# Short down products of two pairs in one section, eight result buffers, goals formed between two pairs' stores

## What is computed

```python
top_p, top_i = jax.lax.top_k(probs, TOPK)                 # 8 experts, 2 for each token
h1 = jnp.einsum('nc,efc->enf', xf, expert_fc1)            # 176 hidden columns
h2 = jnp.einsum('nc,efc->enf', xf, expert_fc2)
out_e = jnp.einsum('enf,ecf->enc', silu(h1) * h2, expert_proj)
y = jnp.einsum('ne,enc->nc', combine, out_e)
s = silu(xf @ shared_fc1.T) * (xf @ shared_fc2.T) @ shared_proj.T
y = y + sigmoid(xf @ shared_gate_w.T) * s
x = x + gb * y
```

## Time and profile before

| | us |
|---|---|
| median of 3 runs | 369.16 (369.09 to 369.76) |
| the profiled execution | 370.18 |
| its span (first to last instruction) | 368.4 |
| PE busy | 353.6 (96%) |
| DVE / ACT / POOL busy | 239.1 / 158.3 / 140.8 |

### The profile page before, as it was taken

One profiled execution on the slowest core, in us unless ns is written; L12 is line 12 of the kernel. 1 busy time (PEld: TensorE's weight loads), 2 busy tenths in 40 slices (PEclk: granted clock), 3 DMA queues, 4 the chain that ended last, 5 costly groups with the idle time before them and its releaser, 6 DMA issues.

```text
span 368.4 us, 9813 instructions
## 1 busy us (share of the span) xinstructions
PE 353.6 (96%) x3793; PEld 218.3 (59%) x3794; DVE 239.1 (65%) x578; ACT 158.3 (43%) x303; POOL 140.8 (38%) x207
## 2 busy tenths in 40 slices
PE   8999999999999998999999999989889999999996
PEld 8445656575656575556845754656556666664464
DVE  3199584998799679756393693136556666665485
ACT  3597628634872622271052411135555555531110
POOL 7706006201712162225363076502465656665000
PEclk9999999999999999999999999999999999999999
DMA  6980300000000000079921062233545554531694
GB/s 194 352 248 5 117 4 3 2 4 4 3 2 4 4 2 4 4 215 285 304 77 59 1 171 80 102 59 72 116 103 117 119 116 103 116 81 45 195 356 135
DMA packets 51660, 36.66 MB, mean 100 GB/s; under 512 B 31447, under 2 KB 48290, under 8 KB 51620
## 3 DMA queue, kind: packets, MB, share of 16 engines
q1 hardware_dynamic: 48212, 27.58, 28.3%
q0 software_dynamic: 3408, 8.51, 7.2%
HBM read 18.06 MB, written 13.68 MB: 86 GB/s over the span
## 4 chain that ended last, share of the span: by engine, by line
PE 70%; issue 9%; POOL 6%; SPq 6%; ACT 4%; DMA 2%; DVE 1%; another core or an unknown queue 1%; DVEq 0%; POOLq 0%; ACTq 0%
PE at_ps L1899 9%; PE work L1570 7%; PE at_ps L1521 7%; PE work L1521 6%; POOL xs_sorted L682 4%; SPq L515 4%; PE work L1922 4%; PE work L1711 3%; PE at_ps L1570 3%; PE work L1761 3%; PE work L1924 3%; PE work L1536 2%; PE at_ps L1536 2%; PE at_ps L1608 2%; PE o_even L1664 2%
## 5 line engine op out<-in xcount | busy, mean ns | idle before, releaser
L1899 PE MATMUL at_ps<-arena 128*128 x156 | 54.5, 473 | 1.3 <-DVE arena L1425 1.3
L715 POOL DMA_INDIRECT ys_tokens<-er_pos,goal_u x39 | 39.7, 1018 | 19.7 <-issue 9.1
L682 POOL DMA_INDIRECT xs_sorted<-h2tok,pos_u x32 | 33.0, 1032 | 21.5 <-issue 12.2
L966 ACT ACTIVATE arena<-h2tok 128x512 uint16<-128x512 uint16 x39 | 30.3, 777 | 24.0 <-DMA h2tok<-xs_sorted 23.2
L1899 PEld LDWEIGHTS at_ps<-arena 128*128 128x128 f32 x156 | 26.6, 190 | 16.6 <-issue 8.1
L1445 DVE SCALAR_TENSOR_TENSOR er_pos<-work,goal,sq 128x256 f32<-128x256 f32 x39 | 17.5, 481 | 18.4 <-PE work L1929 11.9
L627 POOL TENSOR_TENSOR arena<-arena 128x512 f32<-128x512 f32 x8 | 10.2, 1281 | 48.7 <-DVE arena L1377 48.7
L621 POOL COPY h2tok<-xn 128x2048 uint16<-128x2048 uint16 x4 | 7.6, 1892 | 48.0 <-DVE xn L1277 32.6
L1521 PE MATMUL work<-h2T,sup_sb 128*128 128x512 f32 x56 | 25.8, 600 | 0.0
L736 ACT ACTIVATE hs<-at_ps 128x512 f32<-128x512 f32 x10 | 6.0, 598 | 43.0 <-PE at_ps L1521 40.2
L1266 DVE COPY_PREDICATED arena<-causal,at_ps 128x512 f32<-128x512 uint32 x32 | 20.5, 725 | 4.0 <-PE at_ps L1608 4.0
(11 more groups left out here) (291 smaller groups left out, 797.8 us busy)
## 6 DMA issues: line engine op xcount, KB each, us to landing
arena<-ys_tokens SPq DMA_DIRECT2D x8, 512.0 KB, 7.7
arena<-in_e_up SPq DMA_DIRECT2D x8, 352.0 KB
x_sb<-in_x SPq DMA_DIRECT2D x4, 512.0 KB, 9.2
out_rows<-x_sb SPq DMA_DIRECT2D x16, 128.0 KB, 2.2
sup_sb<-in_s_up SPq DMA_DIRECT2D x2, 640.0 KB, 4.9
xs_sorted<-state SPq DMA_DIRECT2D x2, 526.0 KB
xs_sorted<-state SPq DMA_DIRECT2D x8, 131.5 KB
hs<-in_wmod SPq DMA_DIRECT2D x1, 1024.0 KB, 7.7
```

The costliest lines, as they stand in the source:

```text
L682: g.indirect_dma_start(out=xs_dram, out_offset=bass.IndirectOffsetOnAxis(ap=pos_u[:, k, t:t + 1], axis=0), in_=h2row[:, t, :], in_offset=N ...
L715: g.indirect_dma_start(out=ys_dram, out_offset=bass.IndirectOffsetOnAxis(ap=goal_u[:, i:i + 1], axis=0), in_=yout[:, q % 2, u, :], in_offs ...
L966: a.activation(xT[:, u % XBUFS, :].bitcast(U16).rearrange("p (k n a) -> p a k n", k=KC, a=2), xp[:, u, :, :].rearrange("p (a k) n -> p a k ...
L1899: ins = t_.matmul(at_ps[2 + u % 2][:, 0:2 * FE], xT[:, u % XBUFS, k * P:(k + 1) * P], eup[:, bass.ds(e, 1), k, :].rearrange("p a n -> p (a ...
```

## The change

Six things are edited.

1. PE: `down` keeps the main products only. Two pairs write into the two halves of each of the banks `work[0]` and `work[1]`; the new `down_short` does the short products of both pairs after the second one's main products, in the order even, odd, even, odd. PE waits for y once for two pairs.
2. DVE: the four y of a block come together behind that section (`out_rows`), in the next pair's iteration, and the four gains of a block together in its second pair's iteration, behind the two products. Gains lie in `xn` (four places), `yout` has eight buffers, each with a semaphore of its own.
3. POOL: `goals(q + 2)` moves from ahead of `put_rows(q)` to between `put_rows(q)` and `put_rows(q + 1)`.
4. ACT: `tail_odd` has four places, so its copy waits for a section two blocks back.
5. SP: the first eight tiles are loaded in the order four planes, four words, four planes, four words.
6. `mod_cols`: each product gets 128 columns (each batch column repeated 64 times), and DVE reads one of each 64.

The diff, cut to its core:

```diff
-        tail_odd = xn2[:, 0:2, :]
+        tail_odd = xn2[:, :, :]
-        row_step, row_gain = sq[:, 0, 0:HID], sq[:, 1, :].rearrange("p (a n) -> p a n", a=2)
-        yout = er_pos[:, :, :].rearrange("p a (t c) -> p a t c", t=2)
+        row_step, row_gain = sq[:, 0, 0:HID], xn
+        yout = [home[:, a, :].rearrange("p (t c) -> p t c", t=2) for home in (er_pos, h2T[:, 0, :, :]) for a in range(2)]
...
@@ sync
-            for u in range(0, EGRP, 2):
-                load_planes(u)
-                load_planes(u + 1)
-                load_words(u)
-                load_words(u + 1)
+            for u in range(0, EGRP, EGRP // 2):
+                for t in range(u, u + EGRP // 2):
+                    load_planes(t)
+                for t in range(u, u + EGRP // 2):
+                    load_words(t)
...
@@ gpsimd
             for q in range(0, EPAIRS, 2):
+                put_rows(q)
                 if q + 2 < EPAIRS:
                     goals(q + 2)
-                put_rows(q)
                 put_rows(q + 1)
...
@@ scalar
-                act.wait_ge(down_full, q - 1)
+                act.wait_ge(down_full, d)
...
-                            odd_rows(q0 + u // 2, u // 2, e[u])
+                            odd_rows(d0 + u // 4 - 1, u // 2, e[u])
...
@@ vector
             def row_gains(i, u):
-                if not isinstance(i, int) or i:
+                if u % 4 == 0 and (not isinstance(i, int) or i):
                     dve.wait_ge(y_out, i)
                 dve.wait_ge(goal_ready, i + 2)
...
-            def evac_y(i0, q0, u):
-                dve.wait_ge(down_full, q0 + u // 2 + 1)
+            def evac_y(i0, d0, u):
+                dve.wait_ge(down_full, d0 + u // 4 + 1)
...
+            def out_rows(i0, d0, u, tiles=4):
+                for n in range(u, u + tiles):
+                    y_slot_free(i0, n)
+                    evac_y(i0, d0, n)
...
                 for u in range(0, tiles, 2):
                     if u or not first:
                         evac_hT(q0 + u // 2 - 1, (u // 2 - 1) % XPAIRS)
                     expert_h(i0 + u, u)
-                    if u or not first:
-                        row_gains(i0 + u - 2 if u else i0 - 2, (u - 2) % EGRP)
                     if u + 1 < tiles:
                         expert_h(i0 + u + 1, u + 1)
-                    for t in range(2):
...
+                    if u == 4:
+                        out_rows(i0, d0, 0)
+                    elif u == 0 and not first:
+                        out_rows(i0 - EGRP, d0 - XPAIRS // 2, 4)
+                    elif u % 4 == 2:
+                        row_gains(i0 + u - 2, u - 2)
+                        row_gains(i0 + u, u)
...
             evac_hT(EPAIRS - 1, XPAIRS - 1)
-            row_gains(ETILES - 1, EGRP - 2)
-            y_slot_free(ESLOTS - EGRP, EGRP - 2)
-            evac_y(ESLOTS - EGRP, ESLOTS // 2 - XPAIRS, EGRP - 2)
+            out_rows(ESLOTS - EGRP, (ESLOTS // 2 - XPAIRS) // 2, 4, tiles=3)
...
@@ tensor
-                            ins = t_.matmul(o[:, (w * KC + h) * BATCH:(w * KC + h + 1) * BATCH], wmod_sb[:, k, c0:c0 + P],
-                                            csil[:, k, :], start=(k == 0), stop=(k == KC - 1))
+                            ins = t_.matmul(o[:, (w * KC + h) * P:(w * KC + h + 1) * P], wmod_sb[:, k, c0:c0 + P],
+                                            csil[:, k, :].unsqueeze(2).broadcast_to([P, BATCH, P // BATCH]),
+                                            start=(k == 0), stop=(k == KC - 1))
...
-                at_least(pe, y_out, i, 0)
+                if w % 2 == 0:
+                    at_least(pe, y_out, i, 0)
+                c = slice(w % 2 * HID, w % 2 * HID + HID)
                 for t in range(tiles):
...
+            def down_short(q, w, e, tiles=4):
+                if tiles == 4:
+                    pe.wait_ge(odd_ready, q + 1)
...
+                for a in range(2):
+                    c = slice(a * HID, a * HID + HID)
+                    ins = t_.matmul(work[0][:, c], hTe[0:FE1, a, 2 * P:3 * P],
+                                    edn[0:FE1, 1, bass.ds(e[2 * a], 1), :].rearrange("p a n -> p (a n)"),
+                                    start=False, stop=True, skip_group_check=True)
+                    if 2 * a + 1 < tiles:
+                        ins = t_.matmul(work[1][:, c], hTe[r, a, 2 * P:3 * P], tail_odd[r, (w - 1 + a) % XPAIRS, :],
+                                        start=False, stop=True, skip_group_check=True)
                 ins.then_inc(down_full, 1)
...
+                def short_behind(u):
+                    if u == 4:
+                        down_short(q0 + 1, 1, e[0:4])
+                    elif u == 0 and before is not None:
+                        down_short(q0 - 1, XPAIRS - 1, before)
...
                     pair_behind(down, u)
+                    short_behind(u)
```

More of the change, by code:

```diff
@@ L387, in adaln_moe @@
         hTp_full, hTe_ready, down_full, y_out, ys_stored = (
-            sem("hTp_full"), sem("hTe_ready"), sem("down_full"), sem("y_out"), [sem(f"ys_st{i}") for i in range(4)])
+            sem("hTp_full"), sem("hTe_ready"), sem("down_full"), sem("y_out"), [sem(f"ys_st{i}") for i in range(EGRP)])
         weights_ready, row_ready, end_ready = sem("weights_ready"), sem("row_ready"), sem("end_ready")
@@ L537, in _ @@
             for j, s in enumerate(ys_stored):
-                sp.wait_ge(s, 16 * len(range(j, ETILES, 4)))
+                sp.wait_ge(s, 16 * len(range(j, ETILES, EGRP)))
             for q in range(NBLK):
@@ L975, in _, with odd_rows, group @@
             ereg = [act.alloc_register(f"odd_expert{u}") for u in range(EGRP)]
-            def odd_rows(q, w, e):
-                act.wait_ge(down_full, q - 1)
+            def odd_rows(d, w, e):
+                act.wait_ge(down_full, d)
                 copy_odd_rows(w, e)
             def copy_odd_rows(w, e):
-                a.activation(tail_odd[CHUNK:CHUNK + FE1, w % 2, :], edn[0:FE1, 0, bass.ds(e, 1), :].rearrange("p a n -> p (a n)"),
+                a.activation(tail_odd[CHUNK:CHUNK + FE1, w, :], edn[0:FE1, 0, bass.ds(e, 1), :].rearrange("p a n -> p (a n)"),
                              ACT.Copy).then_inc(odd_ready, 1)
-            def group(i0, q0, tiles=EGRP, first=False, last=False):
+            def group(i0, d0, tiles=EGRP, first=False, last=False):
                 act.load(ereg, texp_u[0:1, bass.ds(i0, EGRP)])
@@ L994, in group @@
                     if u % 2:
-                        if first and u < 4:
+                        if first:
                             copy_odd_rows(u // 2, e[u])
                         else:
-                            odd_rows(q0 + u // 2, u // 2, e[u])
+                            odd_rows(d0 + u // 4 - 1, u // 2, e[u])
                     if not (last and u + XBUFS - 1 >= tiles):
@@ L1003, in _ @@
             with act.Fori(1, ESLOTS // EGRP - 1) as grp:
-                group(grp * EGRP, grp * XPAIRS)
-            group(ESLOTS - EGRP, ESLOTS // 2 - XPAIRS, tiles=ETILES - ESLOTS + EGRP, last=True)
+                group(grp * EGRP, grp * (XPAIRS // 2))
+            group(ESLOTS - EGRP, (ESLOTS // 2 - XPAIRS) // 2, tiles=ETILES - ESLOTS + EGRP, last=True)
             for f in range(FTS):
@@ L1918, in down @@
                     pe.wait_ge(shev_done, 2 * NBLK - 2)
[L1919 removed]
+                if w % 2 == 0:
+                    at_least(pe, y_out, i, 0)
+                c = slice(w % 2 * HID, w % 2 * HID + HID)
                 for t in range(tiles):
                     main = edn_odd if t else edn[:, 0, :, :]
[L1922 to L1930 removed]
+                    t_.matmul(work[t][:, c], hTe[:, w % 2, t * P:(t + 1) * P],
+                              main[:, bass.ds(e[t], 1), :].rearrange("p a n -> p (a n)"),
+                              start=(w % 2 == 0), stop=False, skip_group_check=True)
+            def down_short(q, w, e, tiles=4):
+                if tiles == 4:
+                    pe.wait_ge(odd_ready, q + 1)
+                else:
+                    pe.wait_ge(odd_ready, q)
+                r = slice(CHUNK, CHUNK + FE1)
+                for a in range(2):
[6 more added lines that the diff above has]
+                                        start=False, stop=True, skip_group_check=True)
                 ins.then_inc(down_full, 1)
@@ L1937, in fetch_experts @@
                 pe.load(ereg, texp_u[0:1, bass.ds(i0, EGRP)])
-            eprev = [pe.alloc_register(f"expert_prev{u}") for u in range(2)]
+            eprev = [pe.alloc_register(f"expert_prev{u}") for u in range(4)]
             def group(i0, q0, before=None, tiles=EGRP, last=False):
@@ L1948, in pair_behind @@
                     elif before is not None:
-                        step(i0 - 2, q0 - 1, XPAIRS - 1, before)
+                        step(i0 - 2, q0 - 1, XPAIRS - 1, before[2:4])
+                def short_behind(u):
[3 more added lines that the diff above has]
+                        down_short(q0 - 1, XPAIRS - 1, before)
```

(6 more changed lines are left out.)

40 lines of the change are left out of this document (13 added, 27 removed).

## The result

The changed kernel takes 374.38 us (median of 4 runs, 373.68 to 374.52) where the kernel before takes 369.12 (4 runs, 368.13 to 369.76): a ratio of 1.0129, 95% interval 1.0098 to 1.0161. It is slower, by less than 2%. (All ratios are formed over the runs in the fast state, and so need not be the quotient of the two medians, here 1.0143.) The profiled execution after took 373.68 us with a span of 371.9, so the two spans differ by 3.5 us. The granted clock of TensorE is 1.0 in both, from the first slice on.

What follows compares the result with a forecast made beforehand. TensorE bounds the kernel before at 8.78 us a block; afterwards a four-engine ring of 9.37 would bind. Loop, tail and reload delays end 3.3 later: 369.16 + 3.3 = 372.5 us, range 368.3 to 376.0.

Steps and rivals of the forecast that it cites:

- the ring (part 2): Experts' loop: result, two stores, goals, gains, copy, mains, shorts, result close a circle of 9.37 us a block.
- part 1: Short passes of two pairs in one section: 0.40 us less per two pairs, 4.0 us in all on PE.
- part 4: SP's first loads: first PE gap closes, pair 3 at 256.4 against 256.58, nothing gained; ends -1.0 and +0.5.
- first stretched ring: Start of the loop: second block's y at about 266.9, not 266.0, behind tile 11's late planes: +0.8 us.
- The tail: After the last pair: gains wait for goals; shared product 8.9 behind the pair, now 8.1; first reload at 348.2.
- the sum: Whole kernel: the delays of loop, tail and reload added up, putting the end 3.2 to 3.3 us later.
- part 3: Eight result buffers: DVE's wait of 1.48 us for a store's landing goes.
- part 5: Sixteen first-column passes widened from 2 to 128 columns: cost 0, bounds -0.1 to +0.4 us.
- A: Rival: goals come in time, PE stays the bound at 8.38 a block, 364 us; 0.15 with cases between it and D.
- B: Rival: "remote" stall of 1.49 recurs or reload lands at 7.7, not 5.5: 374 to 377 us; 0.14 with C.
- C: Rival: short passes don't stream, 0.32 each, ring grows by 0.2 a block: 374.1 us; 0.14 together with B.
- D: Rival: ring shorter by 0.3 to 0.5 a block, 368.5 to 370 us, about no change; 0.07.

Runs made afterwards that it cites:

- e1: Changed kernel with the next block's goals formed ahead of the block's four stores: 368.35 us, 0.9916 of the kernel before.
- e2: Changed kernel with the next block's goals formed behind all four stores: 405.15 us, 1.0909 of the kernel before.
- e3: Changed kernel with a block's four gains formed later on VectorE, behind the copy and first product: 366.36 us, 0.9872 of the kernel before; repeated, 0.9923.
- e6: e3 with the short passes in two sections a block again, as in the kernel before: 368.79 us, 0.9910 of the kernel before.
- e7: e3 with four result buffers in place of eight: 367.08 us, 0.9876 of the kernel before.
- e11: e3 with the words of tiles behind the first eight loaded by ScalarE in place of SyncE: 367.13 us, 0.9939 of the kernel before.
- e4: e1 with two short sections a block again: 373.34 us, 1.0045 of the kernel before.

## Why the prediction was right, point by point

- **The bound and the ring (part 2)** were right, in mechanism and in size. By the terms of the prediction, beside the rows after: y to the second store's end and the goal 4.49 (1.26 + 2.24 + 0.99 forecast, 4.49 measured, 299.58 - 295.09); the goal itself 0.21; hand-over 0.07 forecast, 0.11 measured; gains 1.60, measured 1.59 (301.49 - 299.90); copy to mains 0.71, measured 0.70; mains to shorts 1.06, the same; four shorts 0.75, the same; last short to y 0.48, measured 0.52. Sum 9.37, this block 9.43, all eight 9.46. e1, e2 and e3 show that this ring, and nothing else of the change, made it slower.
- **The packed section (part 1)**: passes at 0.21 to 0.22 us behind the first, a section of 1.06 and a TensorE bound of 8.38, all as costed from the earlier trace rows. The whole gain of 4.0 us was too high, though: with the ring open e6 gives 1.9.
- **Pair 3** was put at 256.4 and came at 256.90. The step that failed is "the first gap on PE closes" in part 4. It did not:

```profile
246.71 0.69 DVE L1205 TENSOR_TENSOR x_sb<-x_sb,tmp 128x512 f32<-128x512 f32 x1
...
247.32 0.58 DVE L1425 TENSOR_TENSOR arena<-at_ps,arena 128x176 f32<-128x176 f32 x2
247.90 1.45 PE L1902 MATMUL at_ps<-arena 128*128 x4 [1.27 <-DVE arena L1425]
```

Not the planes held it: TensorE waits for the first pair's product (L1425), which stands in VectorE's queue behind an addition of the shared part (L1205). The gap is 1.27 us before and after.

- **The first stretched ring** was put at +0.8 and measures 9.63 - 9.46 = 0.2. The last pair was due at 331.4 + 0.8 = 332.2 and came at 332.49. That this fits so well is luck: pair 3 came 0.5 late, the first ring was 0.6 shorter than written, and the other blocks were each a little longer than 9.37, so that pairs 3 to 19 take 75.59 where 75.76 was due.
- **The tail**: last main 7.25 after the pair, measured 7.28 (339.77 - 332.49); shared products 8.9, measured 8.97; first reload 348.2, measured 347.66, because the term "store to reload 3.1" measures 2.23 (347.66 - 345.43); combine 353.7, measured 353.17, 5.5 after the reload as taken. VectorE waited 0.34 us for it, which TensorE had in hand. So the step that failed here is the 0.5 us that the sum adds for the reload: the reload was not what ended last, and TensorE's own lateness of 2.95 (2.7 forecast) carried to the down products and to the last result.
- **The end**: 3.3 later forecast, 3.5 in the spans of the profiled executions, of which 0.55 stands at the last stores, a term that the sum does not have; it takes the place of the reload's 0.5 by luck. The medians lie 5.3 apart, since the profiled run before was 1.1 above the median of its kernel and the one after 0.7 below. So the forecast was 2.0 us too small, and the rows, from one execution of each kernel, explain 3.5 us of the 5.3.
- **Buffers (part 3)**: the wait of 1.48 is gone, and e7 shows that the buffers are not needed for the speed of e3.
- **First columns (part 5)**: cost 0, as said, and against the rule of the Trainium skill (TensorEngine Tiling (Array Packing), section Instruction Overhead) the wide passes are no longer (0.11 us each, with 2 and with 128 columns). But the step "0, bounds -0.1 to +0.4" missed a gain: the clock behind the narrow passes.
- **Rivals**: A's condition, that no copy waits for a goal, is what e1 and e3 made; A's 364 was too low, since even e3 takes 366.4. B's price is near the median, but neither of its causes came: no gap of the loop names "remote", and the reload landed in 5.5. C fell with the rows of the short passes, D with blocks of 9.46.

## What to carry to other kernels

When work is merged into larger steps, add up the circle from a result through every queue back to the work that it releases, at the new step's size; an order that costs nothing for a pair can close a ring for a block. Then look for the one instruction in an in-order queue that need not stand there: here four gains moved behind a copy and a product turned 1.013 into 0.987 (0.992 when repeated). A side effect on the first microseconds, as on the clock, is found only by looking at the windows there.

## What the hardware showed that I had not expected

- A wait of TensorE inside a dense stretch can be paid a second time, and its length alone doesn't tell whether it will. Behind the gap of 1.90 in e1 the mean clock of ten microseconds is 0.83 and four products take 2.47 in place of 1.45 us; with the 1.88 in e11 it is 0.57 from 269 to 273 us, and with the 3.53 in e2 0.51 from 304 to 311. But behind a longer gap in e2, 2.26 us ahead of 267.21, it stays at 1.00, as it does behind the 2.15 ahead of 318.57 and behind the gaps of 0.56 to 0.99 in the changed kernel:

```profile
268.00:272.00 4.00, 4.00 (x21) 2.55 (x20) 2.41 (x6) 1.51 (x3) 1.06 (x1) 1.00 0.43 85
```

- Sixteen passes of 2 columns take as long as sixteen of 128 (1.89 and 1.95 us at a clock of 1.00), and after the narrow ones the mean clock of two microseconds may be 0.59.
- Waits whose releaser is named "remote" hold the copy up for as long as 1.5 (before), 1.9 (e1) and 2.5 us (e4) in traces of kernels with the goals ahead of the stores (before, e1, e4), and in no trace with the goals between them. Their cause is open.
